# Two half-width parts for the first 64 batch rows of an xDeepFM-like kernel

## What is computed

```python
e = emb_table[feat_index]                       # 512 x 39 x 16
flat = e.reshape(512, -1)
linear_part = flat @ linear_w + linear_b
h1 = relu(einsum('bhd,bmd,ohm->bod', e, e, conv_w1) + conv_b1[None, :, None])
nxt, hi1 = split(h1, 2, axis=1)
h2 = relu(einsum('bhd,bmd,ohm->bod', nxt, e, conv_w2) + conv_b2[None, :, None])
res = concatenate([hi1, h2], axis=1).sum(axis=2)
y = relu(bn(flat @ deep_w1 + deep_b1)); y = relu(bn(y @ deep_w2 + deep_b2))
return concatenate([linear_part, res, y], axis=1) @ out_w + out_b
```

## Time and profile before

| | us |
|---|---|
| Median of 3 runs (lowest, highest) | 467.68 (466.58, 468.43) |
| Profiled execution, its own time | 468.59 |
| Its span, first to last instruction | 466.8 |
| PE busy | 405.0 |
| DVE busy | 356.1 |
| POOL busy | 325.3 |
| ACT busy | 192.7 |

### The profile page before, as it was taken

One profiled execution on the slowest core, in us unless ns is written; L12 is line 12 of the kernel. 1 busy time (PEld: TensorE's weight loads), 2 busy tenths in 40 slices (PEclk: granted clock), 3 DMA queues, 4 the chain that ended last, 5 costly groups with the idle time before them and its releaser, 6 DMA issues.

```text
span 466.8 us, 4589 instructions
## 1 busy us (share of the span) xinstructions
PE 405.0 (87%) x1240; PEld 230.1 (49%) x1240; DVE 356.1 (76%) x365; ACT 192.7 (41%) x241; POOL 325.3 (70%) x234
## 2 busy tenths in 40 slices
PE   0001949899899999999999999999999999989986
PEld 0000514454455555556555555555556565565562
DVE  5121626779858898899879787999876888899994
ACT  1113032224441652275237423734455347576443
POOL 5787777557786758886889888834469268639662
PEclk9999988899999999999999999999999999999999
DMA  3857949967999997999999979997976999999920
GB/s 63 145 84 142 181 56 205 233 165 170 241 236 246 216 228 183 220 235 244 229 215 230 234 179 224 233 236 203 238 182 141 233 227 221 235 242 249 253 58 2
DMA packets 42558, 90.51 MB, mean 194 GB/s; under 512 B 16044, under 2 KB 21483, under 8 KB 42532
## 3 DMA queue, kind: packets, MB, share of 16 engines
q1 hardware_dynamic: 28797, 80.80, 71.6%
q10 hardware_dynamic: 8615, 8.09, 7.6%
q0 software_dynamic: 5120, 1.32, 6.5%
HBM read 88.90 MB, written 1.28 MB: 193 GB/s over the span
## 4 chain that ended last, share of the span: by engine, by line
PE 58%; DVE 11%; POOL 9%; issue 8%; DMA 8%; ACT 3%; SPq 1%; ACTq 1%; DVEq 0%; POOLq 0%
PE p_h L820 34%; PE p_n L820 15%; POOL G L526 6%; PE p_x L800 6%; DVE ring L661 5%; DMA xa<-xs_scratch 3%; DMA ring<-xs_scratch 2%; POOL zl L540 2%; PE p_x L887 2%; DMA G<-in_emb,idx_all 1%; DVE placed L661 1%; DVE zl L630 1%; SPq L513 1%; PE p_n L859 1%; ACT zh L1006 1%
## 5 line engine op out<-in xcount | busy, mean ns | idle before, releaser
L540 POOL TENSOR_TENSOR zl<-ring,zh 128x1024 fp32r<-128x1024 f32 x61 | 144.7, 2387 | 81.3 <-ACT zh L1006 77.0
L526 POOL DMA_INDIRECT G<-in_emb,idx_all x160 | 163.2, 1020 | 49.7 <-issue 40.4
L661 DVE TENSOR_TENSOR ring<-p_n,ring 128x1024 f32<-128x1024 f32 x147 | 174.6, 1217 | 13.7 <-ACT p_n L1032 10.4
L1006 ACT ACTIVATE zh<-ring 128x1024 fp32r<-128x1024 f32 x81 | 85.2, 1056 | 131.9 <-DVE ring L661 124.5
L820 PE MATMUL p_h<-ring,w2s 128*128 128x512 f32 x264 | 125.3, 607 | 6.6 <-DVE ring L661 5.4
L820 PE MATMUL p_n<-placed,w1s 125*128 125x512 f32 (+2 forms) x192 | 91.7, 602 | 0.0
L661 DVE TENSOR_TENSOR placed<-xa,p_x 125x1024 f32<-125x1024 f32 (+2 forms) x45 | 54.8, 1217 | 38.8 <-PE p_x L800 35.2
L820 PEld LDWEIGHTS p_h<-ring,w2s 128*128 128x128 f32 x264 | 50.8, 193 | 56.3 <-issue 44.6
L820 PE MATMUL p_h<-zh,w2l 128*128 128x512 f32 x180 | 69.3, 466 | 1.2 <-ACT h2s L1040 1.2
L800 PE MATMUL p_x<-stack,put 103*125 103x512 f32 (+3 forms) x116 | 51.8, 528 | 12.7 <-DVE stack L635 9.7
L820 PE MATMUL p_h<-zh,w2h 128*128 128x512 f32 x180 | 56.6, 395 | 0.0
(11 more groups left out here) (110 smaller groups left out, 291.2 us busy)
## 6 DMA issues: line engine op xcount, KB each, us to landing
ring<-xs_scratch SPq DMA_DIRECT2D x294, 256.0 KB, 6.8
xa<-xs_scratch ACTq DMA_DIRECT2D x21, 156.0 KB
G<-in_emb,idx_all POOLq DMA_INDIRECT x160
x<-xs_scratch ACTq DMA_DIRECT2D x14, 156.0 KB
xs_scratch<-xT ACTq DMA_DIRECT2D x16, 64.0 KB
dw_sb<-in_dw SPq DMA_DIRECT2D x4, 200.0 KB
xa<-xs_scratch SPq DMA_DIRECT2D x3, 156.0 KB
xa<-in_dw ACTq DMA_DIRECT2D x2, 156.2 KB
```

The costliest lines, as they stand in the source:

```text
L526: nc.gpsimd.indirect_dma_start(G[:, b % 2, DIM * f:DIM * (f + 1)], None, emb[:, :], bass.IndirectOffsetOnAxis(idx_all[:, b, f:f + 1], 0)). ...
L540: nc.gpsimd.tensor_tensor(low_of(s), z_of(s), high_of(s).bitcast(F32), ALU.subtract).then_inc(s_low_pool, 1)
L661: nc.vector.tensor_tensor(z_of(s), by, x, ALU.mult).then_inc(s_z, 1)
L1006: nc.scalar.activation(high_of(s), z_of(s), ACT.Copy).then_inc(s_zh, 1)
```

## The change

The first 64 rows become two parts of 32 rows; there are now 9 parts and 234 positions in `SEQ` in place of 208. A part of 32 rows has 512 columns, and its gathers hold four groups of 10 fields on the 128 partitions, so that it needs 10 of them. Their indices are brought into that layout by four small loads, two of them on SP and two on ACT. Block 1 is now part 2, and so on. Every function takes widths and offsets of its part (`TOK_OF`, `CHUNKS_OF`, `FROM`).

`x2` is gone: `stack` is made from the first 39 rows of `xa`, by two ACT copies; the first third of `xa` has a load and a semaphore of its own. PE's first placement of a part waits for both copies. In the two half parts `flatT` isn't filled by ACT but by 12 loads from the scratch tensor (`load_flat`); these and the 24 loads of the dense layers' weights and small constants (`load_deep`) are issued by SP behind the first ring load of stage 3. The biases of the two interaction layers keep their place in SP's queue, with a semaphore of their own. Eight gathers of part 2 are issued ahead of the loop, its other twelve one for every 700 columns that are multiplied. The tables of the order are new in stages 0 to 2, and in the later ones mostly shifted by one stage. The buffers of placed tiles are four in place of three.

```diff
+HALVED = 1
+HALVES = 2 * HALVED
+ROWS_OF = [ROWS // 2] * HALVES + [ROWS] * (BLOCKS - HALVED)
+PARTS = len(ROWS_OF)
+FROM = [sum(ROWS_OF[:b]) for b in range(PARTS)]
+TOK_OF = [DIM * r for r in ROWS_OF]
+CHUNKS_OF = [t // BANK for t in TOK_OF]
+GROUPS = [128 // r for r in ROWS_OF]
+PER_GROUP = [2 * HALF_F // g for g in GROUPS]
+FLAT_FIELDS = [[8, 2] if g == 4 else [8, 8, 4] for g in GROUPS]
...
-X_AT = {0: [6, 7, 10, 11, 15, 16], 1: [4, 9, 10, 12, 14, 16], 2: [0, 2, 5, 8, 10, 13], 3: [0, 2, 5, 8, 10, 13],
-        4: [0, 2, 5, 8, 10, 13], 5: [0, 4, 7, 9, 12, 14], 6: [0, 2, 4, 6, 8, 10], 7: []}
-P_AT = {0: [4, 24, 25], 1: [21, 23], 2: [20, 25], 3: [17, 20, 25], 4: [17, 20, 25], 5: [], 6: [], 7: []}
+X_AT = {0: [5, 7, 10, 13, 17, 18], 1: [5, 8, 9, 14, 15, 20], 2: [3, 8, 9, 15, 16, 18], 3: [0, 2, 4, 8, 10, 13],
+        4: [0, 2, 5, 8, 10, 13], 5: [0, 2, 5, 8, 10, 13], 6: [0, 4, 7, 9, 12, 14], 7: [0, 2, 4, 6, 8, 10], 8: []}
+P_AT = {0: [22], 1: [24], 2: [1, 22, 23], 3: [17, 20, 25], 4: [17, 20, 25], 5: [17, 20, 25], 6: [], 7: [], 8: []}
...
-DVE_LOW = {-1: [], 0: [2, 8, 12, 25], 1: [1, 6, 15, 23], 2: [16, 20, 25], 3: [20, 25], 4: [20, 25], 5: [1, 8, 15, 16],
-           6: [1, 12, 19, 22], 7: [0, 2, 9, 10, 17, 23]}
-POOL_LOW = {-1: [], 0: [13], 1: [5, 8, 11, 17, 21], 2: [1, 3, 7, 11, 21, 24], 3: [1, 3, 7, 11, 16, 21, 24],
-            4: [1, 3, 7, 11, 16, 21, 24], 5: [3, 5, 11, 13, 17, 19, 21, 22, 23, 24, 25],
-            6: [5, 7, 9, 11, 14, 15, 16, 18, 20, 21, 23, 24, 25], 7: [-1, 3, 4, 5, 6, 7, 8, 11, 12, 13, 14, 16, 18, 22]}
+DVE_LOW = {-1: [], 0: [1, 12, 22], 1: [10, 11, 13, 24], 2: [6, 13, 14, 23, 25], 3: [20, 25], 4: [20, 25], 5: [20, 25],
+           6: [1, 8, 15, 16], 7: [1, 12, 19, 20, 22, 25], 8: [0, 2, 9, 10, 17]}
+POOL_LOW = {-1: [], 0: [], 1: [], 2: [4], 3: [1, 3, 7, 11, 16, 21, 24], 4: [1, 3, 7, 11, 16, 21, 24],
+            5: [1, 3, 7, 11, 16, 21, 24], 6: [3, 5, 11, 13, 17, 19, 21, 22, 23, 24, 25],
+            7: [5, 9, 11, 14, 15, 16, 18, 21, 23, 24], 8: [3, 4, 5, 6, 7, 11, 12, 13, 14, 16, 18, 22]}
...
-T_AT = {0: 14, 1: 9, 2: 6, 3: 6, 4: 6, 5: 5}
-LOW_X_ON_DVE = [3]
-T1_PE, T1_ACT, XA1_ACT, HIGH_X1_ACT, LOW_X1 = (-1, 4), (-1, 2), (-1, 5), (0, 2), (0, 2)
+T_AT = {0: 15, 1: 12, 2: 5, 3: 6, 4: 6, 5: 6, 6: 5}
+LOW_X_ON_DVE = [1, 2, 3, 4]
+FIRST_GATHER, GATHER_COLUMNS, PACED, GATHER_PLACE, GATHER_TILES = 0, 700, 3, 2, 23
+T1_PE, T1_ACT, HIGH_X1_ACT, LOW_X1 = (-1, 0), (-1, 1), (0, 3), (0, 2)
...
-RING, PLACED_RING, HIGH_RING, LOW_RING = 8, 3, 6, 7
-FIRST_LOADS = 5
+RING, PLACED_RING, HIGH_RING, LOW_RING = 8, 4, 6, 7
+FIRST_LOADS = 2
...
-            for at in (0, HIGH_AT):
-                eng.dma_start(x2[at:at + FIELDS, :], xs_rows(b * FIELDS, FIELDS, 1)).then_inc(s_x2, 16)
+        def load_first_x(eng, b):
+            eng.dma_start(xa[0:FIELDS, b % 2, 0:TOK_OF[b]], xs_rows(b, 0, FIELDS, 1)).then_inc(s_first_x, 16)
+
+        def load_xa(eng, b):
+            cols = slice(0, TOK_OF[b])
+            for g in range(1, 3):
+                eng.dma_start(xa[FIELDS * g:FIELDS * (g + 1), b % 2, cols], xs_rows(b, 0, FIELDS, 1)).then_inc(s_xa, 16)
+            eng.dma_start(xa[3 * FIELDS:, b % 2, cols], xs_rows(b, 0, EXTRA, 1)).then_inc(s_xa, 16)
+
+        def load_flat(eng, b):
+            for c, p, first, fields in FLAT_PIECES:
+                src = bass.AP(xs.tensor, xs_at(b, first), [[ROWS_OF[b], DIM * fields], [1, ROWS_OF[b]]])
+                eng.dma_start(flatT[p:p + DIM * fields, c, FROM[b]:FROM[b] + ROWS_OF[b]], src).then_inc(s_flat, 16)
+
+        def load_half_indices(eng, block, g):
+            r, n = ROWS_OF[0], PER_GROUP[0]
+            half, quarter = divmod(g, 2)
+            src = idx[ROWS * half:ROWS * (half + 1), block, n * quarter:n * (quarter + 1)].rearrange("(c r) f -> r c f", c=2)
+            eng.dma_start(idx_raw[r * g:r * (g + 1), block, :].rearrange("r (c f) -> r c f", c=2), src).then_inc(s_idx, 16)
...
-            sp.dma_start(idx_raw[:, :, :], idx).then_inc(s_idx, 16)
+            for g in range(2):
+                load_half_indices(sp, 0, g)
...
+            sp.dma_start(idx_raw[:, HALVED:, :], idx[:, HALVED:, :]).then_inc(s_idx, 16)
...
+                if m == FIRST_LOADS:
+                    own_wait(sp, s_xs, XS_LANDED[1])
+                    load_first_x(sp, 1)
+                    load_xa(sp, 1)
...
+                if j == HALVES + 1 and LOADED[m - 1] < L2_OF[j][0]:
+                    for b in range(HALVES):
+                        load_flat(sp, b)
+                    load_deep()
...
-                for f in range(HALF_F):
+                for f in range(PER_GROUP[b]):
                     gather(b, f)
...
-            dve.wait_ge(s_idx, 16)
+            dve.wait_ge(s_idx, 16 * (4 * HALVED + 1))
...
-                nc.scalar.activation(stack[:, b % 3, :], x2[:, :], ACT.Copy).then_inc(s_high_x, 1)
+                x = xa[0:FIELDS, b % 2, 0:TOK_OF[b]]
+                nc.scalar.activation(stack[0:FIELDS, b % 3, 0:TOK_OF[b]], x, ACT.Copy).then_inc(s_high_x, 1)
+                nc.scalar.activation(stack[HIGH_AT:STACK, b % 3, 0:TOK_OF[b]], x, ACT.Copy).then_inc(s_high_rows, 1)
```

More of the change, by code:

```diff
@@ L142, in order_of @@
     tiles = []
-    for n in range((X_TILES if j < BLOCKS - 1 else 0) + L2_TILES):
+    for n in range((X_TILES if j < PARTS - 1 else 0) + L2_TILES):
         if n in xs:
@@ L153 @@
 SEQ, AT, WHERE = [], {}, []
-for _j in range(-1, BLOCKS):
+for _j in range(-1, PARTS):
     for _n, _tile in enumerate(order_of(_j)):
@@ L159 @@
 INDEX = {tile: s for s, tile in enumerate(SEQ)}
-LAST_X = [INDEX['x', j, X_TILES - 1] for j in range(BLOCKS)]
-FIRST_X = [INDEX['x', j, 0] for j in range(BLOCKS)]
-L2_OF = [[s for s, tile in enumerate(SEQ) if tile[0] in 'pd' and tile[1] == j] for j in range(BLOCKS)]
+LAST_X = [INDEX['x', j, X_TILES - 1] for j in range(PARTS)]
+FIRST_X = [INDEX['x', j, 0] for j in range(PARTS)]
+L2_OF = [[s for s, tile in enumerate(SEQ) if tile[0] in 'pd' and tile[1] == j] for j in range(PARTS)]
 DVE_SPLITS = [s for s, (j, n) in enumerate(WHERE) if n in DVE_LOW[j]]
@@ L444, in each @@
             return [(at, lambda b=b: work(b)) for b, at in (table.items() if isinstance(table, dict) else enumerate(table))]
-        def scratch_write(eng, b, parts):
-            for q, half, fields in parts:
-                halves = 2 if half is None else 1
-                half = half or 0
-                row = b * FIELDS + FLAT_FIELDS[0] * q + HALF_F * half
-                dst = bass.AP(xs.tensor, row * TOK, [[ROWS, DIM * fields], [HALF_F * TOK, halves], [1, ROWS]])
-                eng.dma_start(dst, xT[0:DIM * fields, q, half:half + halves, :]).then_inc(s_xs, 16)
@@ L523, in _, with index_of @@
         def _(pool):
+            def index_of(b, f):
+                if b < HALVES:
+                    at = PER_GROUP[b] * (b % 2) + f
+                    return idx_all[:, b // 2, at:at + 1]
+                return idx_all[:, b - HALVED, f:f + 1]
             def gather(b, f):
@@ L826, in contract @@
                     w = (w1s if layer == 1 else w2s)[0:r, t, :]
-                    for c in range(CHUNKS):
+                    for c in range(CHUNKS_OF[b]):
                         last = mm(c, w, z_of(s), first, final)
@@ L915, in _ @@
                 for b, (j, n) in T_PE.items():
-                    if b > 1 and b not in transposed and AT[T_ACT[b]] < s:
+                    if b > 1 and b not in transposed and AT[T_ACT[b][0], 0] + T_ACT[b][1] < s:
                         transposed.add(b)
@@ L942, in _ @@
         def _(sc):
+            for block in range(HALVED):
+                for g in range(2, 4):
+                    load_half_indices(nc.scalar, block, g)
             load_w1(nc.scalar, w1b_sb, w1b)
@@ new lines, in out_of_transposes @@
+                if b >= HALVES:
+                    rows = slice(FROM[b], FROM[b] + ROWS)
+                    for q in range(2):
+                        nc.scalar.activation(flatT[:, 2 * q:2 * q + 2, rows],
+                                             room_of_t(b)[:, 128 * q:128 * (q + 1)].rearrange("p (a b) -> p a b", a=2), ACT.Copy)
+                    nc.scalar.activation(flatT[0:64, 4, rows], room_of_t(b)[0:64, 256:256 + ROWS], ACT.Copy)
+                    nc.scalar.activation(flatT[64:FLAT_TILES[4], 4, rows], room_of_t(b)[0:FLAT_TILES[4] - 64, 256 + ROWS:256 + 2 * ROWS],
+                                         ACT.Copy).then_inc(s_te, 1)
```

341 lines of the change are left out of this document (185 added, 156 removed).

## The result

Over 20 runs of each, the changed kernel takes 466.04 us and the kernel before 468.37; the ratio is **0.9962, interval 0.9944 to 0.9979**. That is 0.4% faster, within the 0.5% that I had named as the limit of what can be told, and far from the 458 that I predicted; it is just above my range, which ended at 466. One of the changed kernel's runs took 555.49 us at a granted clock of 0.77, and the ratio leaves it out. A second comparison gave 465.04 against 467.65, 0.9934 (0.9911 to 0.9958). The profiled execution took 465.85 us, its span is 463.7, 3.1 us less than the span before.

What follows compares the result with a forecast made beforehand. PE was taken to bound the kernel from 82 us on, with idle time to fill before that. Terms -12.8 + 2.5 = -10.3 gave 458.3 us profiled, 457.4 for the median, stated as 458; 8-in-10 range 451 to 466.

Steps and rivals of the forecast that it cites:

- first product: Start: PE's first product at 34.6 us, 11.1 us earlier, with ACT's w2h rather than gathers holding it.
- block 1's transposes: PE arrives near 59 us and waits until 61.6, when gather 40 lands.
- next stage's first contraction: End of the first 64 rows' layer 2: 112.5 us against 125.3 before, 12.8 us won.
- more PE work later: Stages from block 1's layer 2 on: fewer low parts outside the tail tiles, so PE does 2.5 us more.
- moved DMAs: Stage 3: 36 issues stop ring loads for 16.5 us, covered by tiles in the ring; without cover up to 5 us.
- end of the kernel: End of the kernel keeps its shape: 0 us, bounds -1.5 to +2.
- ring loads: Half stages: a half tile's two 128 KB loads take 1.2 us, between bounds of 1.08 and 1.88.
- DVE: Half stages: products in half widths cost DVE 4.7 us in all, hidden behind PE, with narrow cover.
- rival C: Loads pace both half stages, say 2.2 us per half tile: 467 us, no change; chance 0.08.
- 7 us of idle time: PE after block 1's transposes: two evictions at 1.2, 2.5 for the lower clock, 2 for late fields or tiles.
- rival B: Block 1's fields come late, costing 3 to 6 us more: 463 us; chance 0.15, counted with late weights or index loads.
- D: PE's clock stays low from the first product on, 15 us lost against 10.3 won: 473 us; chance 0.07.

Runs made afterwards that it cites:

- the spread kernel: The changed kernel with its 36 moved loads issued one behind each later ring tile instead of as one block; 460.23 us, ratio to the kernel before 0.9821.
- the second profile: The changed kernel as it is, profiled again in the second comparison, where it took 465.04 us.
- the one with early rectification: The spread kernel with ACT's second and third rectification of part 1 put at position 23 of stage 0; 460.00 us, ratio to the kernel before 0.9821.
- The kernel before, with its own block of loads: The kernel before with its 24 weight and constant loads moved behind block 2's first ring load; 472.01 us (1.0073), on the odd chip 492.53 (1.0040).

## Why the prediction was wrong

Step by step, against the profiled execution:

| step | predicted | measured |
|---|---|---|
| first product | 34.6 | 35.0 |
| block 1's transposes | 61.6 | 61.58 |
| next stage's first contraction | 112.5 | 113.7 |
| gain by then | 12.8 | 11.6 |
| more PE work later | 2.5 | 2.6 (1.9 in stage 2, 0.7 in stage 3) |
| moved DMAs | 0 (up to 5) | 5.4 |
| end of the kernel | 0 (-1.5 to +2) | 0.8 |
| sum | -10.3 | -3.1 |

The measured sum goes by the evictions, whose first gain is 11.9. The 0.7 and the 5.4 share out stage 3's 6.1 by the spread kernel, whose stage 3 is 0.7 us longer than before's. The row of more PE work holds lengths of stages, not busy time: in stage 2 PE is busy 1.1 us longer (47.92 against 46.78), and the other 0.8 are idle. By busy time it is 1.1, 0.7 and, in all that follow, 0.6: 2.4 in sum, so the size was right, and most of the last row's 0.8 is such work too.

*Start, ring loads, DVE: right.* ACT's w2h held the first copy, as said; 128 KB loads came in time (DVE waits for ring loads 6.2 us in nine waits over the whole kernel), so rival C is not seen. To the rule of the Trainium skill, *DMA: Bandwidth & Descriptors*, section "Bandwidth", that transfers be batched to 1 MiB, the trace adds that halving the 256 KB loads cost next to nothing with several in the queue: in stages 0 and 1 DVE waits for one of them once, 0.23 us. After block 1's transposes I had put 7 us of idle time, and 6.2 are there (1.06, 3.59, 1.51). The 3.59 looks like rival B in small, but of its counterpart in the spread kernel (2.49) 1.9 us went when ACT's rectification came earlier, with the fields loaded as late as before: most of it is the order on ACT and not late fields. The granted clock is 1.00 from 60 us on (0.89 from 45 to 60), so D is not seen.

**The step that failed is "Moved DMAs"**, in its word "covered". Its sizes were right: 36 issues took 17.0 us (I said 16.5), and PE did not run out of ring tiles; DVE's first wait for one in that stretch is 0.82 us at 162.74. (For a ring load I took 5 us from issue to landing; the page of the kernel before has a median of 6.8. With it the cover is 23.3 of 26, and still holds.) But I had asked only what PE wants from SP's queue. Two things were left out. First, DMA was at share 1.00 in that stretch, so a transfer put off isn't free: with 105 GB/s for 10 us in place of the 216 that the kernel before moves from 150 to 160, some 1.1 MB had to be moved later, two ring tiles. Second, that catching up meets, if they come soon behind it, the scratch writes of another queue, on which ACT waits in order with PE's copies behind it. What I put at nothing cost 5.4 us (4.4 by the second profile; 4.8 came back in the runs). My upper bound of 5 was nearly the price; I had tied it to the wrong condition, that the ring runs dry, and so gave it no chance of its own. In the list of what would show me wrong, "a hole on PE in stage 3 (moved DMAs)" is what came.

*End: a size.* The 0.8 us (0.3 in the last stage but one, 0.4 in the last) is within the bounds I gave.

## What to carry to other kernels

Work that is moved to "a place with slack" has to be held against the resource, not only against the engine that waits for it: where DMA is full, a long block of small loads leaves a backlog, and the one who pays is the latency-bound chain if it comes soon behind, here a write, its landing, a read, on another queue. Issue such loads one behind each large one; that alone made 465.0 into 460.2, ahead of both kernels; of all versions measured only the one with early rectification is level with it (460.0). And in an engine that works in order, look for the wait on a DMA that has finished work of others queued behind it.

## What the runs showed of the hardware that I had not expected

- SP issues the changed kernel's small loads almost without a pause (0.25 to 0.60 us each), yet DMA's share falls to 0.50 and its rate to 105 GB/s for 10 us (0.99 and 211 in the window before): small loads at that pace don't fill it.
- From 120 us on, with ring loads in flight, the time from the scratch writes of a whole block (156 KB) to the load that waits for them was 6.5 to 15.6 us in the profiles from the usual chips; the longest had no block of small loads near it, and its cause is open.
- On one of the chips used, transfers and engines other than POOL stand for some 10 us at a time while POOL's gathers go on at 1.25 us each: 40 GB/s from 80 to 120 us in the spread kernel, where the same kernel elsewhere moves 193 from 80 to 117. PE (10.7 us idle before 93.33) and DVE (14.3 before 107.54) wait there for nothing that the profile names, so it isn't shown what stands first. PE then drops to the lower clock level (granted 0.50 in one such stretch). The kernel before, with its own block of loads, has such a stand there as well (PE idle 11.6 us before 69.02), but fewer. I didn't find the cause.
